# Sharing the quantisations of the first layer between VectorE and ScalarE in a Flamingo-style kernel

## What is computed

```python
def bitnet_linear(x, W, b):            # the first cross-attention and its network
    w_scale = jnp.maximum(jnp.mean(jnp.abs(W)), 1e-05)
    qW = jnp.sign(W) * (jnp.abs(W) > 0.5 * w_scale).astype(W.dtype)
    i_scale = jnp.maximum(jnp.max(jnp.abs(x)), 1e-08) / 127.0
    qx = jnp.clip(jnp.round(x / i_scale), -128.0, 127.0)
    out = jnp.einsum('...i,oi->...o', qx, qW) * (w_scale * i_scale)
    return out + b

# the gated network of the first layer; act_qdq rounds to 16 bits with one scale,
# fixed_qdq_u16 rounds to 1/65536 and clips to 65535/65536
gate = act_qdq(gate * sig)             # sig = fixed_qdq_u16(sigmoid(gate))
o = act_qdq(gate * up)
return o @ lpbq_dequant(w_down).T
```

## Time and profile before

| what | value |
|---|---|
| median of three runs | 1121.85 us (1125.45, 1121.85, 1108.79) |
| profiled execution | 1109.89 us, span 1108.1 us |
| TensorE busy | 763.3 us, 69% |
| VectorE busy | 702.7 us, 63% |
| ScalarE busy | 435.6 us, 39% |
| GpSimd busy | 283.8 us, 26% |
| chain that ended last | TensorE 48%, VectorE 28%, GpSimd 7%, issue 6%, DMA 5%, ScalarE 4% |

### The profile page before, as it was taken

How to read it: one execution, slowest core, us unless ns; L and a number is a source line. 1 busy time by engine, 2 the same in 40 slices (tenths; PEclk the granted TensorE clock), 3 DMA queues, 4 the chain that set the end, 5 groups by cost and what they waited for, 6 DMA issues and landing times.

```text
span 1108.1 us, 22943 instructions
## 1 busy us (share of the span) xinstructions
PE 763.3 (69%) x8188; PEld 634.6 (57%) x8191; DVE 702.7 (63%) x1706; ACT 435.6 (39%) x969; POOL 283.8 (26%) x326
## 2 busy tenths in 40 slices
PE   0427427206898496499977699955899998649980
PEld 0315213005676495377767699943677786639770
DVE  5866786896476532668767555646777767463334
ACT  1423405512444264246544333323454444216550
POOL 1000000000000276055551577620000000037771
PEclk9759768557899699599998799987999999759995
DMA  7400000000600112800001111136000000101114
GB/s 192 124 0 2 1 0 1 0 0 8 166 0 1 50 54 64 249 1 0 1 1 39 32 47 47 46 113 152 2 1 0 0 0 2 39 21 51 52 51 126
DMA packets 72966, 48.07 MB, mean 43 GB/s; under 512 B 19546, under 2 KB 65636, under 8 KB 72900
## 3 DMA queue, kind: packets, MB, share of 16 engines
q1 hardware_dynamic: 64484, 31.80, 10.8%
q0 software_dynamic: 6464, 13.25, 3.8%
q10 hardware_dynamic: 1952, 2.15, 0.7%
HBM read 33.74 MB, written 13.43 MB: 43 GB/s over the span
## 4 chain that ended last, share of the span: by engine, by line
PE 48%; DVE 28%; POOL 7%; issue 6%; DMA 5%; ACT 4%; ACTq 0%; DVEq 0%; POOLq 0%; SPq 0%; another core or an unknown queue 0%
PE ps L2116 9%; PE ps L2130 5%; PE ps L1960 4%; PE ps L1605 4%; POOL rows_y L552 3%; PE ps L1900 3%; POOL arena L547 3%; PE ps L1913 2%; PE ps L1856 2%; PE ps L1873 2%; PE ps L1617 2%; DMA rows_y<-arena,row_out 2%; DVE x L1218 2%; DVE bst L576 2%; PE ps L1777 2%
## 5 line engine op out<-in xcount | busy, mean ns | idle before, releaser
L2116 PE MATMUL ps<-arena 128*128 128x128 f32 x1120 | 149.1, 284 | 0.8 <-DVE arena L1153 0.4
L547 POOL DMA_INDIRECT arena<-rows_x,row_in x101 | 99.9, 989 | 178.3 <-DVEq L1199 148.5
L2116 PEld LDWEIGHTS ps<-arena 128*128 128x128 f32 x1120 | 138.5, 198 | 2.6 <-issue 1.7
L2130 PE MATMUL ps<-arena 128*128 x808 | 110.9, 281 | 8.2 <-DVE arena L1167 7.7
L552 POOL DMA_INDIRECT rows_y<-arena,row_out x101 | 104.6, 1035 | 42.8 <-issue 20.1
L1605 PE MATMUL ps<-q,onesb 128*128 128x256 bf16 x523 | 78.4, 289 | 48.5 <-DVEq L859 48.5
L2130 PEld LDWEIGHTS ps<-arena 128*128 128x128 f32 x808 | 99.3, 194 | 13.8 <-issue 13.5
L1153 DVE COPY arena<-arena 128x644 f32 (+1 forms) x101 | 62.3, 617 | 63.5 <-DVE arena L1167 31.3
L885 DVE TENSOR_REDUCE arena<-ps 128x8 f32<-128x512 f32 (+1 forms) x96 | 57.3, 597 | 55.5 <-PE ps L1873 36.7
L1408 ACT COPY arena<-ps 128x512 f32<-128x512 f32 (+1 forms) x96 | 46.4, 515 | 111.1 <-PE ps L1900 111.1
L1554 ACT ACTIVATE arena<-ps,arena 128x128 f32<-128x128 f32 x248 | 70.9, 368 | 44.7 <-PE ps L2116 44.7
(11 more groups left out here) (296 smaller groups left out, 1594.6 us busy)
## 6 DMA issues: line engine op xcount, KB each, us to landing
arena<-rows_y SPq DMA_DIRECT2D x20, 256.0 KB, 4.7
arena<-in_L_ffn_w SPq DMA_DIRECT2D x2, 2048.0 KB, 9.0
arena<-in_L_ffn_w SPq DMA_DIRECT2D x16, 256.0 KB, 6.5
rows_x<-xh SPq DMA_DIRECT2D x3, 1024.0 KB, 5.1
rows_x<-zero SPq DMA_DIRECT2D x1, 2560.0 KB, 10.9
arena<-in_L_ffn_gate_proj SPq DMA_DIRECT2D x8, 256.0 KB, 5.0
arena<-in_L_ffn_up_proj SPq DMA_DIRECT2D x8, 256.0 KB, 5.2
arena<-in_L_ffn_down_proj SPq DMA_DIRECT2D x1, 2048.0 KB, 10.0
```

Of the source, the lines that this page charges most:

```text
L547: g.indirect_dma_start(xq[:, q % XS, :], None, rows_x, bass.IndirectOffsetOnAxis(row_in[:, q:q + 1], 0)).then_inc(sem(f"xq_loaded{q % XS}" ...
L2116: ins = pe.matmul(ps[:, 2 * m + s_ % 2, P * f:P * f + P], wst[:, s_ % 4, lo:lo + P], xqT[:, s_ % 2, :], start=True, stop=True)
L2130: ins = pe.matmul(ps[:, 4 + s_ % 2, 0:P], hT[:, s_ % 2, f, :], w2[:, P * f:P * f + P], start=(f == 0), stop=(f == NF - 1))
```

## The change

A constant `SHARE = 1344` splits the columns of each quantisation: VectorE takes columns 0 to 1343, ScalarE the 704 others, with the same two steps. ScalarE starts on a semaphore `scale_open`, which VectorE increments once `irecip` is written, and VectorE waits for `act_quant`, which ScalarE increments with its last operation. This is done for the tokens (`qtok`), for act0 twice, for `fused`, and for the four parts of `h0`, where it is TensorE that waits for both. Of the two functions below the first is VectorE's and the second ScalarE's. The context's quantisation at L679 and the small `qavg` stay with VectorE.

```diff
+            def quantise_shared(dst, src, scratch):
+                v.sem_inc(sem("scale_open"), 1)
+                quantise(dst[:, 0:SHARE], src[:, 0:SHARE], scratch[:, 0:SHARE])
+                k_shared[0] += 1
+                v.wait_ge(sem("act_quant"), k_shared[0])
...
+            def quantise_shared(dst, src, scratch, scale):
+                own.wait()
+                s.wait_ge(sem("scale_open"), scale)
+                k_shared[0] += 1
+                own(s.activation(scratch[:, SHARE:2048], src[:, SHARE:2048], ACT.Identity, bias=magic[:, 0:1],
+                                 scale=irecip[:, 0:1]))
+                own.wait()
+                s.activation(dst[:, SHARE:2048], scratch[:, SHARE:2048], ACT.Identity, bias=no_magic[:, 0:1]
+                             ).then_inc(sem("act_quant"), 1)
```

The sum and the scaling of `avg` move behind the announcement of `qT_ready`, and the bias of f2 is added to x before the maxima of h0 and no longer behind them:

```diff
-            own(v.tensor_reduce(avg[:, :], act0.rearrange("p (b s) -> p b s", s=S), AX.X, ALU.add))
-            quantise(qT, act0, rnd)
+            quantise_shared(qT, act0, rnd)
             out_scale(3, 3)
             out_scale(0, 4)
             own.wait()
+            v.sem_inc(sem("qT_ready"), 1)
+            own(v.tensor_reduce(avg[:, :], act0.rearrange("p (b s) -> p b s", s=S), AX.X, ALU.add))
+            own.wait()
             own(v.tensor_scalar(avg[:, :], avg[:, :], 1.0 / S, None, ALU.mult))
             own.wait()
-            v.sem_inc(sem("qT_ready"), 1)
...
+            v.sem_inc(sem("scale_open"), 1)
             for f in range(NF):
-                own.wait()
-                own(v.tensor_scalar(h0[:, f, :], h0[:, f, :], irecip[:, 0:1], MAGIC, ALU.mult, ALU.add))
-                own.wait()
-                v.tensor_scalar(qh[:, f, :], h0[:, f, :], MAGIC, None, ALU.subtract).then_inc(sem("qh_ready"), 1)
+                quantise(qh[:, f, 0:SHARE], h0[:, f, 0:SHARE], h0[:, f, 0:SHARE])
+            own.wait()
+            v.sem_inc(sem("qh_ready"), NF)
```

In the gated network ScalarE takes MAGIC off the sigmoid and scales it back, after its roundings of `up0`, and VectorE applies the cap in the product itself. The first third of the two later requantisations is rounded in halves of 1024 columns, the first by VectorE and the second by ScalarE, ahead of its roundings of the other thirds. The last piece below is ScalarE's:

```diff
-                own(v.tensor_scalar(sig0[:, f, :], sig0[:, f, :], MAGIC, 65535.0, ALU.subtract, ALU.min))
-                own.wait()
-                own(v.scalar_tensor_tensor(gate0[:, f, :], sig0[:, f, :], 1.0 / 65536.0, gate0[:, f, :],
-                                           ALU.mult, ALU.mult))
+                own(v.scalar_tensor_tensor(gate0[:, f, :], sig0[:, f, :], 65535.0 / 65536.0, gate0[:, f, :],
+                                           ALU.min, ALU.mult))
...
+            def requantise_halves(buf, rounded, name=None):
+                for c in range(2):
+                    h = buf[:, 1024 * c:1024 * c + 1024]
+                    if c:
+                        v.wait_ge(sem("rounded"), rounded)
+                    else:
+                        own(v.tensor_scalar(h, h, irecip[:, 0:1], MAGIC, ALU.mult, ALU.add))
+                        own.wait()
+                    ins = v.tensor_scalar(h, h, MAGIC, iscale[:, 0:1], ALU.subtract, ALU.mult)
...
             for n, buf in enumerate((up0, gate0, gate0)): 
                 s.wait_ge(sem("scale_ready"), n + 1)
+                if n:
+                    s.activation(buf[:, 0, 1024:2048], buf[:, 0, 1024:2048], ACT.Identity, bias=magic[:, 0:1],
+                                 scale=irecip[:, 0:1]).then_inc(sem("rounded"), 1)
                 for f in range(1, NI):
                     s.activation(buf[:, f, :], buf[:, f, :], ACT.Identity, bias=magic[:, 0:1], scale=irecip[:, 0:1]
                                  ).then_inc(sem("rounded"), 1)
+                if n == 0:
+                    own.wait()
+                    for f in range(NI):
+                        s.activation(sig0[:, f, :], sig0[:, f, :], ACT.Identity, bias=no_magic16[:, 0:1],
+                                     scale=1.0 / 65536.0).then_inc(sem("sig_ready"), 1)
```

44 lines of the change are left out of this document (34 added, 10 removed).

## The result

The changed kernel takes 1109.7 us (median of 20 executions, 1102.85 to 1115.39), the kernel before, run beside it on the same chip, 1117.93 us (20 executions, 1108.79 to 1126.1). The ratio is 0.9938 with a 95% interval from 0.9913 to 0.9963. The ratio leaves out executions more than 1.5% above the fastest of their kernel, so it need not be that of the medians, which are 8.2 us (0.7%) apart. By the ratio the change saves 0.6%, where the prediction had 1.15% (1103 us against the same middle before). The profiled execution after took 1103.28 us with a span of 1101.4 us, so against the profiled one before it saves 6.6 us and not 12.8.

A forecast was written before the change was run, and what follows sets the result against it. VectorE's path between scale and announcement was taken to bound the first layer, with ScalarE idle there. Terms 1.9 + 2.3 + 2.25 + 2.65 + 3.05 + 0.4 + 0.25 = 12.8 us gave 1097.1 to 1109.0, middle 1103 us, range 1092 to 1114.

The forecast's parts named there:

- the sum: All claimed savings in the first layer added up: 12.8 us, with bounds from 10.5 to 14.
- single quantisations: qtok, act0 twice, fused: TensorE starts 2.33 us behind the reciprocal instead of 2.77, saving 1.9 us together.
- the average: Average of act0 moved behind the announcement, covered by TensorE's value products up to 0.1 us: saves 2.3 us.
- the bias of x: Moved from between last maximum and scale of h0 into VectorE's idle time: saves 2.25 us, or 1.75 if maxima fall behind.
- h0: Four shared parts: TensorE starts f2 7.35 us behind the last scaling instead of 10.01, saving 2.65 us.
- the sigmoid's wait: Gated network: ScalarE takes MAGIC off first, VectorE's first product waits 0.65 us for it; whole term saves 3.05 us.
- the halves: gate0's quantisation split between VectorE and ScalarE: 2.4 us from reciprocal to L855 instead of 2.80, saving 0.4 us.
- The last term, 0.25: Before the down projection, ScalarE's other roundings slip earlier; between 0 and 0.39 us, taken as 0.25 for the lower clock.
- The middle: Forecast median of 1103 us, between 1097.1 and 1109.0 us, 1.2% below the same middle before; chance 0.72.
- The hand-over's price: Rival: ScalarE's share ends last everywhere, each hand-over costing 0.4 us more; saving 9.9 us, 1106 us; chance 0.12.
- The second rival: Faster by over 2%, helped by stages meeting TensorE's clock rise at another point in the first layer; chance 0.13.
- The third rival: Slower by over 2%: clock falls in a later always-busy stretch, such as 644 to 672 us; about 1125 us; chance 0.03.

The follow-up runs named there:

- The first layer alone: Kernels before and changed, each with layers 1 to 3 left out, 5 executions each: before 286.98 us, changed 274.29 us.
- the two moves: Average and bias of x put in new places; with layers 1 to 3 left out, only these 284.62 us, changed kernel lacking them 276.18 us.
- the warm pair: Changed kernel and kernel before, both with unused filler matmuls in TensorE's idle stretches of the first layer: 1101.89 and 1114.42 us.
- late_start: Changed kernel with its first reduction, 1.75 us on the context, made twice: 1109.41 us, ratio to before 0.9931.
- after: First profiled trace of the changed kernel against the kernel before: this execution took 1103.28 us, median of 20 is 1109.7 us.
- after_again: The changed kernel run once more, nothing else changed, for a second trace: 1108.8 us, ratio to before 0.9908.
- gated_only: Kernel before with only the gated network's change (sigmoid's constant on ScalarE, and the gate0 halves): 1116.33 us, ratio 0.9984.
- warm_moves: Kernel before with the average and the bias of x moved, plus filler matmuls in TensorE's first-layer idle stretches: 1113.58 us, ratio 0.9952.
- warm_before: Kernel before with filler matmuls in TensorE's idle stretches of the first layer: 1114.42 us, ratio 0.9968.

## Why the prediction was off

**What bounds the kernel.** Right for the edited places. VectorE's path between scale and announcement was the bound, and ScalarE could take part of it.

**The prices.** Right to 0.03 us everywhere: 0.97 and 0.88 us for the 704 columns (0.955 and 0.874), 0.92 and 0.86 for the 1344 (0.916 and 0.860), 1.24 for ScalarE's 1024 (1.22), 0.75 for VectorE's. The rule of the Trainium skill, page "ScalarE: Activation LUTs", section "Rules for kernel authors", to use VectorE for additions and products, would have left 4.6 us of the sum. The first layer alone gained 12.5 us, and 10.5 us of it without the two moves, so the rule does not bind where ScalarE is idle and only takes a share that ends with VectorE's.

**The terms.** Each was found in the trace after: single quantisations 2.35 us to TensorE (2.33), the average covered, the bias of x off the chain, h0 7.42 (7.35), the sigmoid's wait 0.68 (0.65), the halves 2.40 (2.4). The sum of 12.8 us is what the first layer alone gains (12.5) and what the warm pair differs by (12.7). The last term, 0.25, is within the clock's play: from the last scale's partial maximum to the first x of the down projection it is 14.0 us before and 14.1 after in the first layer alone, and 14.35 and 14.0 in the profiled whole kernels.

**The step that failed** is the sentence "The layers 1 to 3 have no edit. They start when the first layer ends and wait for nothing tied to the program's start, so what is gained here should arrive whole.", together with an earlier one, "So in this layer a microsecond off VectorE's path between a scale and its announcement is a microsecond off the kernel". Both take every stage behind a term to be of fixed length. First, already in the profiled first layer only 10.2 of 12.8 us came, and 9.9 on average over the traces. Groups of TensorE that follow the gained time start at the lower clock and run longer: the scores 3.44 us for 2.09, and the gate and up products 19.4 to 19.5 us for 17.43 in every trace of the changed kernel without fillers there. The sum had this price at nothing, except for its term of 0.25 us. Second, stages without an edit behind the first layer are not of one length: layer 2's experts take 165.0 to 167.6 or 171.8 to 174.0 us, layer 3's 152.6 to 154.3 or 158.7 to 158.8. How much of the missing gain is lost there stays open. A division by the groups of times can be made (38 of 118 executions before are of the fast kind and 2 of 32 after, which would be 2.9 of the 9.0 us), but it rests on two executions and on a grouping that is weak. That the share depends on where the first layer's end puts these stages is not shown either: `late_start` moved that end by less than a microsecond (260.27 against 259.47), so it was no test of a larger shift.

**The middle.** "I see no row that says which side a median will fall on, and predict the middle, 1103 us". The prediction took the profiled 1109.89 us and 1108.79 for one side of a pair and 1121.85 and 1125.45 for the other. The median before in 20 executions was 1117.93, so the middle of 1116 was low by 2, and with the saving short by 4 to 5 us (8.2 by the medians) the two add up to the 6.7 us between 1103 and 1109.7. The time itself stayed in the range of 1092 to 1114.

**The rivals.** The hand-over's price was not the cause: it costs what the prediction said, and the shares end within 0.1 us of each other at the tokens and at act0, and within 0.2 us at the last part of h0. The second rival had the right mechanism, TensorE's rise met at another point, with the wrong sign: "stages that begin 3 to 13 us earlier may meet its rise at another point" was listed only as what could help. The Trainium skill, "TensorE: Matmul & The Clock Gate", section "What's actually happening", says that the rise depends on where the first matmul lands and moves from run to run. The prediction said that no run showed that yet. That it moves from run to run these do: the first score group of the changed kernel, the same 64 matmuls, in `after` and in `after_again`:

```profile
85.80 2.08 PE L1767 MATMUL ps<-arena 128*64 128x64 f32 x64 [2.33 <-DVE arena L742]
...
85.71 3.58 PE L1767 MATMUL ps<-arena 128*64 128x64 f32 x64 [2.24 <-DVE arena L742]
```

What decides it no run here shows. The third rival, a stretch that loses its clock in the middle of dense work, shows in none of the stretches read; its price was also added up wrong, since 1103 us and 35 us more are 1138 and not 1125.

## What to carry to other kernels

A term read from a bounded path is worth its sum only as far as nothing behind it has two speeds: where TensorE starts after an idle stretch, let the range hold the price of the lower clock for each such group (2 us for 40 products here), and expect stages without an edit to differ by several microseconds between executions. To price a small edit, run the part of the program that holds it alone (12.5 us with an error of 0.8 from 5 executions a side), but compare the clock of its groups with the whole program's: here it was another (19.14 us for 17.43), and the whole first layer gained 9.9. Take the profiled execution for one draw. Filler matmuls in TensorE's idle stretches were worth as much here (10 us) as moving work off the busy engine.

## What the hardware showed unexpectedly

- One kernel on one core spreads by 1.9% (1108.79 to 1129.62 us, 127 executions on several chips; 1110.59 to 1128.16 in one batch of 29 on one chip), and the time of an execution goes with its mean granted clock (correlation -0.94 over 20 executions of the changed kernel).
- The first mark of the program comes at 36.0 to 36.3 us in every trace of a whole kernel that has the two new constants, `gated_only` among them (`late_start`, whose start is longer, is left out), and at 36.8 to 37.2 us in every one that has not. The two memsets and two tiles of one column each also shift later buffers. What of it saves the 0.6 us was not tried, and in the first layer alone nothing is saved (44.1 us before, 44.5 after).
- With fillers ahead of layer 2's transposes, the last of them 22 small matmuls (2.58 us) that end 0.72 us before, the granted clock of the next 16 us is 1.00, where an idle stretch of 5.57 us left them at 0.52.
- Fillers do not make it sure: the first block of the down projection takes 5.47 us in `warm_moves` and 3.84 in `warm_before`, each 1.44 us behind the same fillers.
